# Attention's preparation: remainders subtracted by TensorE in PSUM, and loads split by who reads them

## The reference, cut to what matters

```python
x = x + _L0_attn_a_ref(_layernorm(x), ...)      # a0
# inside, for b1 alike:
q, k, v = heads(x @ Wq), heads(x @ Wk), heads(x @ Wv)
q, k = rope(q), rope(k)
scores = einsum(q, k) / sqrt(hd);  scores = where(causal, scores, -inf)
y = softmax(scores) @ v;  out = y @ Wo + b_out
```

## Time and profile before

| what | value |
|---|---|
| median of 3 runs | 2225.22 us (2221.39 to 2228.47) |
| the profiled execution | 2220.95 us, its span 2219.1 us |
| mean granted TensorE clock | 0.888 of full speed |
| PE / DVE / ACT / POOL busy | 82% / 52% / 33% / 22% |

### The profile page before, as it was taken

How to read it: one execution, slowest core, us unless ns; L and a number is a source line. 1 busy time by engine, 2 the same in 40 slices (tenths; PEclk the granted TensorE clock), 3 DMA queues, 4 the chain that set the end, 5 groups by cost and what they waited for, 6 DMA issues and landing times.

```text
span 2219.1 us, 32673 instructions
## 1 busy us (share of the span) xinstructions
PE 1817.6 (82%) x10328; PEld 1016.5 (46%) x10329; DVE 1150.6 (52%) x2341; ACT 722.2 (33%) x1396; POOL 494.1 (22%) x840
## 2 busy tenths in 40 slices
PE   6699999998489994757999497699467999976992
PEld 4344444432356663544666355376243444344761
DVE  7688888872412215751122456143376887462423
ACT  2277777765111110111111101022023667610220
POOL 2222222221300005621000500500441222133022
PEclk9599999997799996868999698799786999987996
DMA  3331111122200002001000310223223211002322
GB/s 97 83 124 41 42 41 39 38 95 106 81 26 24 19 21 90 1 22 35 24 24 21 116 52 3 88 93 101 66 62 73 37 34 24 1 27 80 99 91 80
DMA packets 97291, 123.35 MB, mean 56 GB/s; under 512 B 19704, under 2 KB 77976, under 8 KB 96408
## 3 DMA queue, kind: packets, MB, share of 16 engines
q1 hardware_dynamic: 87960, 96.67, 15.0%
q0 software_dynamic: 9216, 25.18, 3.5%
HBM read 78.35 MB, written 42.86 MB: 55 GB/s over the span
## 4 chain that ended last, share of the span: by engine, by line
PE 68%; DVE 13%; issue 9%; another core or an unknown queue 4%; POOL 3%; DMA 2%; ACT 1%; SPq 0%; POOLq 0%; DVEq 0%; ACTq 0%
PE psum L1331 12%; PE psum L981 9%; PE psum L965 7%; PE psum L1352 6%; PE psum L929 6%; DVE region_a L778 5%; PE psum L1566 5%; PE psum L1538 3%; PE psum L347 2%; POOL y_norm L1226 2%; PE psum L1769 2%; PE psum L1584 2%; PE psum L1585 2%; PE psum L1341 1%
## 5 line engine op out<-in xcount | busy, mean ns | idle before, releaser
L778 DVE TENSOR_REDUCE region_a<-psum 128x1 f32<-128x640 f32 (+7 forms) x576 | 527.9, 953 | 94.5 <-PE psum L934 54.6
L866 ACT ACTIVATE region_w<-psum 128x512 f32<-128x512 f32 x864 | 465.7, 600 | 227.1 <-PE psum L965 223.7
L1331 PE MATMUL psum<-region_w,region_a 128*128 x608 | 271.9, 601 | 1.5 <-DVE region_a L1407 1.2
L981 PE MATMUL psum<-region_w,region_a 128*32 128x512 f32 (+3 forms) x2304 | 256.6, 520 | 0.8 <-POOL region_w L681 0.6
L929 PE MATMUL psum<-region_a,y_norm 48*128 48x512 bf16 (+7 forms) x816 | 226.2, 354 | 27.4 <-DVE region_a L778 14.3
L681 POOL TENSOR_SCALAR_AFFINE_SELECT region_w<-region_w 128x512 f32<-128x512 f32 x192 | 121.8, 635 | 462.1 <-ACT region_w L866 457.7
L1226 POOL DMA_INDIRECT y_norm<-result_rows,region_a x64 | 63.0, 985 | 713.9 <-DMA result_rows<-region_a 695.9
L965 PE MATMUL psum<-y_norm,region_a 51*128 51x512 bf16 (+1 forms) x612 | 205.7, 400 | 5.9 <-DMA y_norm<-region_a 4.0
L1331 PEld LDWEIGHTS psum<-region_w,region_a 128*128 128x128 f32 x608 | 114.3, 193 | 132.5 <-issue 132.5
L1414 DVE TENSOR_TENSOR region_a<-psum,region_a 128x512 f32<-128x512 f32 x76 | 52.6, 692 | 215.8 <-PE psum L1331 215.8
L1538 PE MATMUL psum<-y_t,region_w 128*128 128x512 f32 (+1 forms) x192 | 100.1, 676 | 73.9 <-DVE ctx L1657 53.3
(11 more groups left out here) (186 smaller groups left out, 2607.4 us busy)
## 6 DMA issues: line engine op xcount, KB each, us to landing
region_a<-sorted_rows SPq DMA_DIRECT2D x116, 128.0 KB, 2.0
result_rows<-region_a SPq DMA_DIRECT2D x116, 128.0 KB, 1.7
y_norm<-a_q SPq DMA_DIRECT2D x132, 64.0 KB
sorted_rows<-ctx SPq DMA_DIRECT2D x1, 4992.0 KB, 17.2
y_norm<-b_q SPq DMA_DIRECT2D x36, 128.0 KB
region_w<-in_f_wg SPq DMA_DIRECT2D x1, 4096.0 KB, 13.3
region_w<-in_f_wu SPq DMA_DIRECT2D x1, 4096.0 KB, 12.9
region_w<-in_f_wd SPq DMA_DIRECT2D x1, 4096.0 KB, 14.2
```

Of the source, the lines that this page charges most:

```text
L778: dve.tensor_reduce(dst, src, AX_X, ALU.max, negate=True).then_inc(self.ring_done.sem, 1)
L866: act.activation(self.p[col % P_RING][:, :, i % 4, :], c.bank[ST_BANKS[s % 3]].rearrange("p (h t) -> p h t", h=GQ), ACT.Exp, scale=self.sc ...
L981: mm = pe.matmul(c.bank[ACC_BANK][32 * h:32 * h + 32, P * lo:512], self.vp[slot][:, j, :], self.p[col % P_RING][:, h, lo:4, :], start=(j = ...
L1331: mm = pe.matmul(bank[:, :], self.yt[:, f, :], w[:, f, bass.ds(own * self.hidden + 512 * half, 512)], start=(f == 0), stop=(f == FT - 1))
```

## The change

The cuts move from DVE to PE and ACT. The transposes open an accumulation in the bank; ACT casts part 1 from it; PE multiplies part 1 by minus the identity (bf16) and adds that to the bank (`less`, new line 919); ACT casts part 2 from the same bank; PE subtracts it in the same way; ACT casts part 3. So a bank takes three ACT operations (all at new line 832) and two more matmuls of 512 columns, and none of DVE. PE's and ACT's lists are written by quarter of a group, so that these steps stand between the products of the next group. There are five part buffers instead of three. Of the two loads in a0, the rows at partition 64 are loaded first, with `q_in1` and `k_in1`, for which `max_scores` waits; the rows at 0 follow after the stores of n = 6, 7, 8, with `q_in0` and `k_in0`, for which the first of the scores waits. In the loop over units SP waits for `q_in0` and `k_in0` of the unit before.

```diff
-        self.rest = [cx.take([512]) for _ in range(2)]
-        self.parts = [r.take([3, 512], BF16) for _ in range(3)]
+        self.parts = [at.take([3, 512], BF16) for at in (r, r, r, cx, cx)]
...
             if n == 3 * NG // NB - 1:
-                self.first_parts_out(sp)
+                self.parts_stored(sp, n + 1)
                 sp.wait_ge(self.pads.sem, self.pads.at(2 + self.slot_pads * 2))
-                load(0, 0)
-        sp.wait_ge(self.q_in.sem, self.q_in.at(16 * len(self.terms) * len(self.copies)))
-        sp.wait_ge(self.k_in.sem, self.k_in.at(48 * len(self.copies)))
+                load_copy(0, 0, self.max_at)
+            if n == 3 * NG // NB + 2 and self.max_at:
+                load_copy(0, 0, 0)
...
-                for i in range(4):
-                    if i < 3:
-                        cut_first(3 * (g - 1) + i)
-                    if i:
-                        cut_second(3 * (g - 1) + i - 1)
+        for t in range(NT):
+            rotate(t)
...
+        def part(n, i, ready, done):
             rows = P if n % 3 < FT else QK_COLS - D
-            act.wait_ge(self.turned.sem, self.turned.at(n + 1))
-            if n >= 3:
-                act.wait_ge(self.parts_out[n % 3].sem, self.parts_out[n % 3].at(16 * (n // 3)))
+            act.wait_ge(ready.sem, ready.at(n + 1))
+            if i == 0 and n >= PARTS:
+                stored = self.parts_out[n % PARTS]
+                act.wait_ge(stored.sem, stored.at(16 * (n // PARTS)))
+            act.activation(self.parts[n % PARTS][0:rows, i, :], c.bank[4 + n % 4][0:rows, :], ACT.Copy)\
+                .then_inc(done.sem, 1)
...
+        def less(n, i, part, done):
+            rows = P if n % 3 < FT else QK_COLS - D
+            pe.wait_ge(part.sem, part.at(n + 1))
+            pe.matmul(c.bank[4 + n % 4][0:rows, :], c.minus[0:rows, 0:rows], self.parts[n % PARTS][0:rows, i, :],
+                      start=False, stop=(i == 1), skip_group_check=True).then_inc(done.sem, 1)
...
+        for g in range(NG + 1):
+            n = 3 * (g - 1)
+            for q in range(4):
+                if g < NG:
+                    multiply(4 * g + q)
+                if g > 1 and q == 0:
+                    less2(n - 1)
+                if g and q == 0:
+                    turn(n)
+                    turn(n + 1)
+                if g and q == 1:
+                    turn(n + 2)
+                    less1(n)
+                if g and q == 2:
+                    less1(n + 1)
+                    less2(n)
+                if g and q == 3:
+                    less1(n + 2)
+                    less2(n + 1)
+        less2(3 * NG - 1)
...
             if k == 0:
-                pe.wait_ge(self.q_in.sem, self.q_in.at((u + 1) * (16 * len(self.terms) * len(self.copies))))
-                pe.wait_ge(self.k_in.sem, self.k_in.at((u + 1) * (48 * len(self.copies))))
+                pe.wait_ge(self.q_in1.sem, self.q_in1.at((u + 1) * (16 * len(self.terms))))
+                pe.wait_ge(self.k_in1.sem, self.k_in1.at((u + 1) * 48))
```

More of the change, by code:

```diff
@@ L35 @@
 P_RING = 4
+PARTS = 5
 P_AT = 16384
@@ L188, in __init__ @@
         self.consts = c.sem("consts_set")
+        self.minus_set = c.sem("minus_set")
         self.zeros = c.cx_pad[:, NT * D:NT * D + D]
@@ L463, in __init__, with stores, parts_stored @@
             biased=NT)
-        self.parts_out = [self.parts_out0, self.parts_out1, self.parts_out2]
         self.m_in = [self.m_in0, self.m_in1]
-    def all_parts_out(self, eng):
-        for s in self.parts_out:
-            eng.wait_ge(s.sem, s.at(16 * NG))
-    def first_parts_out(self, eng):
-        for s in self.parts_out:
-            eng.wait_ge(s.sem, s.at(16 * NG // NB))
+    def stores(self, n, i):
+        return len(range(i, n, PARTS))
+    def parts_stored(self, eng, n):
+        for i, s in enumerate(self.parts_out):
+            eng.wait_ge(s.sem, s.at(16 * self.stores(n, i)))
     def every_unit(self, eng, unit, ahead=1):
@@ L879, in tensor @@
         pe.wait_ge(self.w_in.sem, self.w_in.at(64))
-        def turn(g):
-            pe.wait_ge(self.qk_done.sem, self.qk_done.at(4 * g + 4))
-            self.ln.ready(pe, NG - 1)
-            for f in range(3):
-                n = 3 * g + f
-                rows = P if f < FT else QK_COLS - D
-                if n >= 4:
-                    pe.wait_ge(self.rest_done.sem, self.rest_done.at(n - 3))
-                for q in range(4):
-                    mm = pe.transpose(c.bank[4 + n % 4][0:rows, P * q:P * q + P],
-                                      self.qk[q][:, P * f:P * f + rows], c.identf[:, :])
-                mm.then_inc(self.turned.sem, 1)
@@ L894, in tensor @@
-        for g in range(NG):
-            self.ln.ready(pe, g)
-            for t in range(4 * g, 4 * g + 4):
-                if t >= 4:
-                    pe.wait_ge(self.rotm.sem, self.rotm.at(3 * (t - 3) if hd == 8 else t - 2))
-                    pe.wait_ge(self.v_done.sem, self.v_done.at(t - 3))
-                for f in range(FT):
-                    mm = pe.matmul(c.bank[t % 4][:, 0:3 * P], c.yt[:, f, P * t:P * t + P], self.w[:, f, :],
-                                   start=(f == 0), stop=(f == FT - 1))
-                mm.then_inc(self.prod.sem, 1)
-            if g:
-                turn(g - 1)
@@ L906, in tensor, with multiply @@
-        turn(NG - 1)
+        def multiply(t):
+            if t % 4 == 0:
+                self.ln.ready(pe, t // 4)
+            if t >= 4:
+                pe.wait_ge(self.rotm.sem, self.rotm.at(3 * (t - 3) if hd == 8 else t - 2))
+                pe.wait_ge(self.v_done.sem, self.v_done.at(t - 3))
+            for f in range(FT):
+                mm = pe.matmul(c.bank[t % 4][:, 0:3 * P], c.yt[:, f, P * t:P * t + P], self.w[:, f, :],
+                               start=(f == 0), stop=(f == FT - 1))
+            mm.then_inc(self.prod.sem, 1)
@@ new lines, in turn @@
+        def turn(n):
+            g, f = divmod(n, 3)
+            rows = P if f < FT else QK_COLS - D
+            pe.wait_ge(self.qk_done.sem, self.qk_done.at(4 * g + 4))
+            if n < 4:
+                self.ln.ready(pe, NG - 1)
+            else:
+                pe.wait_ge(self.part3.sem, self.part3.at(n - 3))
+            for q in range(4):
+                mm = pe.matmul(c.bank[4 + n % 4][0:rows, P * q:P * q + P], self.qk[q][:, P * f:P * f + rows],
+                               c.identf[:, :], start=(q == 0), stop=False, is_transpose=True, skip_group_check=True)
+            mm.then_inc(self.turned.sem, 1)
```

121 lines of the change are left out of this document (68 added, 53 removed).

## The result

The kernel after takes 2209.08 us (median of 5 runs, 2206.99 to 2214.25) beside 2226.23 us for the kernel before in the same measurement (median of 5, 2221.39 to 2228.47). The ratio is 0.9927, with a 95% interval of 0.9912 to 0.9942: faster by 12.9 to 19.6 us, 17.2 by the medians. The prediction said 2210.0 within 2201 to 2219. A second measurement of the unchanged kernel after gave 2211.77 (median of 6) beside 2225.62, 0.9939 [0.9924, 0.9954]: 13.9 us by the medians.

A forecast was written before the change was run, and what follows sets the result against it. DVE and PE's order were taken to bound the preparation, then SP's loads and the store behind them. Gains of 10.8 us in a0 and 3.8 in b1 sum to -14.6, from 2225.22 to 2210.6, stated as 2210, range 2201 to 2219.

The forecast's parts named there:

- a0's groups: First preparation: a group takes 8.7 us, 5.60 of rotation plus a 3.1 wait, set by DVE, where it took 9.75.
- A subtraction: PE's added matmul in the preparation groups: 0.21 us each, six a cycle, with 0.30 as the other end.
- a0's end: After a0's last tile: first maximum at 60.7 for 71.50, gain 10.8 us; load_max wanted at 71.25.
- The step: Reckoning for each place: a0, store 11 at 60.2, unit 1's loads from 60.8; b1, store of n = 6 landed at 1664.8.
- b1: Second changed stretch: PE-bound cycle 8.35 us for 7.90, store landing 6.4, first maximum at 1669.8, gain 3.8.
- the upper end of about 8: b1's gain if the store of n = 6 lands in 3.7 as in a0, until the loads bind.
- The sum: Whole kernel: -10.8 in a0 and -3.8 in b1 make -14.6 us, within -19.9 and -8.
- Rival 1: PE at 1.2 GHz in the preparation, 16.0 us a cycle for 8.7, kernel slower; chance 0.06.
- Rival 2: Unit 0 of a0: something there keeps its absolute time and half the gain is lost, -4 to -7; chance 0.15.
- Rival 3: PE comes to unit 0 at 2.4 GHz, -19 to -23 us in all; chance 0.14, counting a short landing in b1.
- Rival 4: a0's first scores still wait for both copies; changes the time by 2 us, within the range; no chance given.
- the price of the negated identity at the start: PE's first wait delayed by one short ACT operation, 0.3 us; DVE binds there, so nothing, at most 0.4.

The follow-up runs named there:

- the padded kernel: Kernel after with the first half of each group's fourth product done twice on PE, 0.66 us a group; 2157.45 us, one run.
- the turned order: Kernel after with the third bank's transposes ahead of the second product of the next group; 2154.49 us, 0.9934 of before.
- The sixth buffer: Kernel after with six part buffers for five, so n = 11 takes the buffer of n = 5; 2151.07 us, 0.9919 of before.
- the kernel with the split alone: Kernel before with only a0's loads of unit 0 split into two copies, cuts still on DVE; 2220.08 us, 1.0014 of before.
- the run that brings its wait back: Kernel after, but PE's first scores of unit 0 in a0 wait for both copies; 0.9925 of before.
- three that were worth 0.8, 0.4 and 0.8 us: On the kernel after: third bank's transposes earlier, a sixth part buffer, row load between unit 1's two copies; all together 2200.71 us, 0.9894 of before.

## Why the prediction was right

The time is 0.9 us from the forecast, and this closeness is partly luck: the gain was 17.2 us by the medians of the first measurement, 13.9 in the second and 13.7 in the two profiled spans, where 14.6 was the sum. By the trace the terms are these.

- **a0's groups.** Predicted 8.7 us, measured 8.64; the wait before a rotation was 2.98 for 3.1. That DVE's chain binds here and PE has room was shown by the padded kernel (0.66 of PE's time cost 0.25) and by the turned order.
- **A subtraction** was set at 0.21 of PE's time, with 0.30 as the other end. b1's cycle of 8.25, all PE's, leaves (8.25 - 5.32 - 1.47) / 6 = 0.24 for one and its gaps.
- **a0's end.** First maximum 59.97 for 60.7, gain 11.5 for 10.8; row load 71.34 for 71.25, gain 10.7. The 0.7 that the first maximum came early did not reach the row load. SP, to which the prediction gave 1.5 us of slack, had none: DVE had the row copied at 70.10 and SP issued its load 1.24 later, where 0.44 had been the distance before; so the queue cost 0.8. The step let the loads of unit 1 start at 60.8, right behind the last store; they started at 62.31, 1.16 after it, since SP first waits for the second copy to land. (With both copies loaded early that gap was 0.16: 65.50 + 0.64 to 66.30.)
- **Its clock.** That PE would be at 1.2 GHz before the first maximum was not seen, but its price was small: the last tile came 0.45 earlier (53.06 for 53.5), and in its nine casts ACT waited for PE only 0.22 and 0.17 us after the first. b1 has it too: a grant of 1.00 from 1617 to 1646 us and 0.58 from 1650.0 to 1658.4, where the prediction wanted near 1.0 in both preparations.
- **b1.** Cycle 8.25 for 8.35. The store of n = 6 took 6.59 us to let ACT go on, for 6.4. First maximum 4.74 earlier for 3.8. The surplus is not in the groups: ACT went on 38.90 us after the first product, where the step has 1664.8 - 1625.81 = 38.99. It lies behind that, 4.18 us to the first maximum for 5.0. The sixth buffer confirms the step: without that store in the way the first maximum comes 4.1 to 4.4 us earlier, until the loads bind, as the upper end of about 8 was reckoned (4.74 + 4.4 = 9.1).
- **The rule on completion order.** By the Trainium skill ("DMA: Bandwidth & Descriptors", section "Queues, rings and completion order") a semaphore increment lands only after every earlier write of that DMA engine, so a store behind nine loads keeps its long landing wherever it stands. The traces agree: behind b1's nine loads the store took 6.3 us to land before and 6.5 now, ahead of them 3.3.
- **The sum.** The two stretches gained 11.7 and 4.7, together 16.4, less 0.2 at the start; predicted was 14.6. The span shows 13.7. The difference is in the 0.8 of SP's queue, which is most of the -0.9 between a0's first copied row and the third unit's, and in stretches that the prediction held constant: +3.3 at the end of a0, -0.3 in layers 2 to 5, -3.1 in layer 6, -1.5 behind b1's first rows. By its own terms the prediction's lower bound is 11.7 + 8 = 19.7, not 19.9; nothing hangs on it.

**The rivals.** Rival 1 (1.2 GHz in the groups) fell: the grant was 1.00 from 42 to 50 us, where it was 0.79 before. From 28 to 51 us PE never paused for more than 0.32 us, where before it had stood 2.71 ahead of the product at 42.47. The Trainium skill ("TensorE: Matmul & The Clock Gate", section "A second HAM failure mode: psum-queue depth-cycling") warns of such short idling; it did not occur in the groups here, with PE busy 7.63 of 8 us. Rival 2 (the gain stops at the next wait) was at work, but for 0.8 us on SP only; in the kernel with the split alone it took 2.4 of 2.7. Rival 3 (clock up in unit 0) did not come: the grant is 0.50 from 55 to 100 us. Rival 4 was excluded by the run that brings its wait back, at 2.5 to 2.6 us.

What was argued and not tested: the price of the negated identity at the start and the two extra waits of SP in each unit. The first product stood at 19.66 us for 19.48, but at 19.49 in the second execution of the kernel after, so the 0.2 is scatter. The 12 middle units of a0 took the same 319.5 us in both kernels, so the waits cost nothing there. Nor does any run take apart the 6.9 us that a0 gains without the split: the subtraction on PE, the five buffers and the new order of PE's list came together.

## What to carry to other kernels

When work moves between engines, follow the first moment at which the next stage can start, and what each buffer waits for: here it was a store that stood in ACT's way, before the change (4.79 us in a0) and after it (0.73 there, 5.82 in b1), and in b1 one more buffer took it away. An edit that is worth nothing alone (the split of the loads, 1.0014) can be worth 4 us beside another, and three that were worth 0.8, 0.4 and 0.8 us at the next load were worth 4.8 together, because each had ended at a different queue. Compare the length of stretches that nobody touched before crediting a few microseconds to an edit; 3 us came and went here, at the end of a0 with the clock's moment.

## What was not expected of the hardware

- A matmul of the negated identity (bf16, 512 columns) onto a bank that fp32 transposes had opened costs PE about 0.24 us with its gaps at 2.4 GHz, two in a row 0.59 in the record, one alone 0.61 to 0.63 at 1.2 GHz.
- The store behind nine loads released ACT after 6.59 us in b1 and after 3.6 in a0 (52.05 to 55.68), in the new order as in the old (6.41 and 3.66). Issued ahead of the loads in b1, it landed in 3.3.
- The length of layer 6 went from 243.8 to 250.8 us among kernels whose layer 6 is the same code, and was 229.6 to 230.1 in the four kernels of the measurement where the kernel before took 2170.65 us. In those four ACT's last copy of 96 rows came 55.0 us after the first transpose for 68.5 to 74.9 elsewhere, and the remainder was as long as elsewhere (174.5 to 175.1 for 173.8 to 177.0). With the sixth buffer PE stood only 1.98 us in that stretch. From layer 8's first transpose to the end it was 230.9 to 232.7 us there and 258.2 to 267.5 elsewhere. The 12 middle units of a0 agreed within 0.17 us in all of them. What sets this level is open; the record names the same chip for that measurement and for the one where the kernel before took 2216.41.
